# A three-layer graph network kernel: eight groups in flight instead of four, dot products of layers 2 and 3 one slot earlier, small VectorE operations as tensor-tensor

## The chip, the core and the metric

One core of one Trainium2 chip. The time is the device time of one execution in microseconds, from its first to its last instruction with the little that lies around it; the kernel before took 2461.77 us, the median of 3 runs (2460.39 to 2462.76).

## What is computed

128 graphs of 128 nodes with 256 features each. The input is normalized and cut at zero, goes through three graph attention layers, and is added to the untouched input:

```python
mask = adjacency + eye > 0
x = relu(layernorm(x_in))
for l in range(3):
    si, sj = x @ attn_w[l, :d], x @ attn_w[l, d:]
    scores = leaky_relu(si[:, :, None] + sj[:, None, :] + attn_b[l], 0.2)
    attn = softmax(where(mask, scores, -inf))
    h = layernorm(x + attn @ x) * g1[l] + beta1[l]
    ff = gelu(h @ W1[l] + b1[l]) @ W2[l] + b2[l]
    x = layernorm(h + ff) * g2[l] + beta2[l]
return x_in + x
```

## The kernel before, in words

**Items and slots.** Four graphs (T = 4) are one group, and one layer of one group is one item: 32 groups by 3 layers are 96 items. `RING` = 4 groups are in flight: items 0 to 3 are layer 1 of groups 0 to 3, then come four items of layer 2, four of layer 3, and the next four groups. `PER` = 12 items are one round. Every engine runs its own list, written out in Python by `slots`, one slot per item. In slot s every engine goes through c = 0 to 7, the eight blocks of 128 hidden features.

**What a slot holds.** TensorE (`hidden`, L369, and `feed`, L383) does the two large products of item s, each split in fp16 high and low parts; `feed` runs three blocks late (`LAG`), so its last three lie in c = 0 to 2 of the next slot. In between TensorE does small parts of items that come: the aggregation of item s+1 at c = 0 (L425), at c = 4 the transposes of the normalized rows of item s+1 (L435) and the spreading of the s_j of item s+2 (L407), and at c = 7 the transposes of the probabilities of item s+2 (L413).

ScalarE does GELU and the fp16 rounding of each block (L481, L486), the normalization of item s+1 at c = 2 (L491), the high part of X at c = 3 (L528), of hT at c = 4 (L535), at c = 5 the exponentials of item s+2 (`exponentials`: the leaky ReLU L509, then a table load and four exponentials L514), and at c = 7 the normalization of an input.

VectorE does the low part of each block (`g_lo`, L573), after c = 0 the statistics' end of norm 1 (`aggregates`: L585, L587, L588), after c = 1 the eight dot products of item s+2 (`dot_products`, L614 and L617), after c = 2 the residual of the second norm (`feed_residual`, L681), after c = 3 its statistics (L580), after c = 4 the scores (L632), their row maxima (`row_maxima`, L638 and L642) and `aggregates` of norm 2, after c = 5 the low part of hT (L671) and the statistics of an input, after c = 6 the low part of the probabilities and a mask, after c = 7 the residual of the first norm (L656) and its statistics.

GpSimd does, in this order and once per slot: 1/sqrt of norm 1 (`inverse_deviation`, L789 and L791, handed to ScalarE's L491), `h_residual` (L801, L803), the low part of X (`low_X`, L807), 1/sqrt of norm 2, `norm_feed` (four L815), for items of layer 3 the `skip_connection` (L836), for a group that starts 1/sqrt of the input's norm, and `layer_output` (L827, L829, twice).

**What fixes the order.** The lists are written by hand, each engine works through its own in order, and semaphores with computed totals join them. Inputs (`input_statistics`, mask, input normalization) are four slots ahead of their item (`starts`). X of an item in layer 2 or 3 is the output of the item `RING` before it, written by `layer_output` at the end of the slot after that one: with RING = 4, X for item s+3 is the output of item s-1, which is written at the end of slot s. `h_residual` waits, besides its operands, for the dot products of item s+2. The row maxima end in one instruction, `minus_max` = min(0.2 * row_top, row_top), and ScalarE's exponentials wait for it.

SP issues all DMAs in order: weights at the start, then per group the inputs, the store and the second load of x for the skip connection, in buffers used in turn.

Of the kernel before, what the change touches and what calls it, by code (L numbers as in the profile page):

```python
# [41 lines left out]
RING = 4  # L42
# [55 lines left out]

def is_item(r, s):
    return not isinstance(r, int) or 0 <= PER * r + s < ITEMS  # L100
# [29 lines left out]
def gnn_kernel(nc, x, adj, attn_w, attn_b, W1, b1, W2, b2, g1, beta1, g2, beta2, out):  # L130
    with ExitStack() as ctx:
# [12 lines left out]
        minus_half = sb("minus_half", [P, T])  # L144
        w1_f32 = sb("w1_f32", [P, KD, H])
# [21 lines left out]
        x_again = [sb(f"x_again{i}", [P, T, D]) for i in range(2)]  # L167
        y_out = [sb(f"y_out{i}", [P, T, D]) for i in range(2)]
# [106 lines left out]
        def _(sp):  # L275
            def weights(l):
                if l >= 1:
                    sp.wait_ge(w_lo_ready, 4 * l - 2)
                    sp.wait_ge(bias_psum, l)
                sp.dma_start(w1_f32[:], W1[l].rearrange("(k p) h -> p k h", p=P)).then_inc(w_dma[0], 16)  # L280
                if l >= 1:
                    sp.wait_ge(w_lo_ready, 4 * l)
                sp.dma_start(w2_f32[:], W2[l].rearrange("(c p) d -> p c d", p=P)).then_inc(w_dma[1], 16)

            def graphs(tensor, g):

                v = tensor.rearrange("(g t) n d -> n g t d", t=T)
                if isinstance(g, int):
                    return v[:, g]
                return v[:, bass.ds(g, 1)].rearrange("n g t d -> n (g t) d")  # L290

            def load_x(g, i):
                sp.dma_start(x_in[i][:], graphs(x, g)).then_inc(x_loaded[i], 16)

            def load_adj(g, i):
                sp.dma_start(adj_in[i][:], graphs(adj, g)).then_inc(adj_loaded[i], 16)

            def load_again(g, i):
                sp.dma_start(x_again[i][:], graphs(x, g)).then_inc(x_again_loaded[i], 16)

            def store(g, i):
                sp.dma_start(graphs(out, g), y_out[i][:]).then_inc(stored[i], 16)

            load_x(0, 0)
            load_adj(0, 0)
# [7 lines left out]
            load_x(1, 1)  # L313
            load_adj(1, 1)
            weights(0)
            for g in (2, 3, 4, 5):
                sp.wait_ge(x0_ready, 4 * (g - 1))
                load_x(g, g % 2)
                sp.wait_ge(mask_steps, 2 * (g - 1))
                load_adj(g, g % 2)  # L320
                if g == 2:
                    for dst, v in ((g1_rows, g1), (b2_rows, b2), (res_rows, beta1), (g2_rows, g2), (beta2_rows, beta2)):
                        sp.dma_start(dst[:].rearrange("p l d -> p (l d)"),
                                     flat(v).partition_broadcast(P)).then_inc(rows_dma, 16)
                if g in (3, 4):
                    weights(g - RING + 2)
            load_again(0, 0)
            load_again(1, 1)

            for r in range(LOOPS - 1):  # L330
                for q in range(RING):
                    i, g = q % 2, r * RING + q

                    sp.wait_ge(x0_ready, r * (4 * RING) + 4 * (RING + q + 1))
                    load_x(g + (RING + 2), i)
                    sp.wait_ge(mask_steps, r * (2 * RING) + 2 * (RING + q + 1))
                    load_adj(g + (RING + 2), i)

                    sp.wait_ge(x_steps, x_total(r, 2 * RING + q, 5))
                    store(g, i)  # L340
                    load_again(g + 2, i)
            for g in range(RING * (LOOPS - 1), G):
                if g + RING + 2 < G:
                    sp.wait_ge(x0_ready, 4 * (g + RING + 1))
                    load_x(g + RING + 2, g % 2)
                    sp.wait_ge(mask_steps, 2 * (g + RING + 1))
                    load_adj(g + RING + 2, g % 2)
                sp.wait_ge(x_steps, x_total(g // RING, 2 * RING + g % RING, 5))
                store(g, g % 2)
                if g + 2 < G:  # L350
                    load_again(g + 2, g % 2)
# [115 lines left out]
        def _(act):  # L467
# [39 lines left out]
            def exponentials(r, s):  # L507
                act.wait_ge(score_steps, total(r, s, 6, 6))
# [52 lines left out]
        def _(dve):  # L561
# [73 lines left out]
            def row_maxima(r, s):  # L635

                dve.wait_ge(score_steps, total(r, s, 6, 4))
                dve.tensor_reduce(row_top[:], scores[:], AX.X, ALU.max, negate=True).then_inc(score_steps, 1)  # L638
                dve.wait_ge(score_steps, total(r, s, 6, 5))
# [66 lines left out]
            def slot(r, s):  # L706
# [7 lines left out]
                for c in range(C):  # L714
# [35 lines left out]
                    if c == 5 and starts and not late:  # L750
                        input_statistics(r, s + 4)
# [127 lines left out]
```

## Time and profile before

| | |
|---|---|
| median of the runs | 2461.77 us |
| the profiled execution | 2464.22 us, span 2462.4 us |
| busy: TensorE matmul | 2350.7 us (95%) |
| VectorE | 2097.8 us (85%) |
| ScalarE | 1890.0 us (77%) |
| GpSimd | 1701.0 us (69%) |
| DMA | 29 GB/s mean, the queue 9.1% busy |
| granted TensorE clock | 0.993 over the span |

The profiled execution lies 2.4 us above the median of the runs. A matmul's row gives 273 ns where the next one starts 0.11 us later, since matmuls overlap: TensorE's rate is read from the start-to-start times in its timeline, and a gap from the start of the last matmul before it.

### The profile page before, as it was taken

What the parts mean: (1) busy time and instruction counts of PE and PEld (TensorE: products, weight loads), DVE (VectorE), ACT (ScalarE), POOL (GpSimd) and SP (SyncE); (2) the same over time, 40 slices, a digit from 0 to 9 for tenths busy, and PEclk for the clock granted to TensorE, in tenths of its full rate; (3) what the DMA queues carried; (4) which work ended last, traced back from release to release, by engine and by line L of the source; (5) the groups of instructions that cost most, each with busy time, mean ns of one, the idle gap of its engine ahead of it and who ended that gap; (6) DMA issues with size and microseconds to landing.
All of it is one profiled execution on the core that took longest, in us unless ns stands there. A gap on an engine that the chain in (4) does not pass through costs nothing.

```text
span 2462.4 us, 47718 instructions
## 1 busy us (share of the span) xinstructions
PE 2350.7 (95%) x16608; PEld 1648.4 (67%) x16608; DVE 2097.8 (85%) x6070; ACT 1890.0 (77%) x3402; POOL 1701.0 (69%) x1540
## 2 busy tenths in 40 slices
PE   3999999999999999999999999999999999999997
PEld 2766666676666666667666666666666666666765
DVE  6778998888988899888988889988898889988884
ACT  4767788877787878787787777877778777878783
POOL 3457677767776767766786667776678676777675
PEclk9999999999999999999999999999999999999998
DMA  5200012000210002100021001200012000110001
GB/s 170 73 1 1 1 44 78 1 1 1 74 48 1 1 14 61 48 1 1 14 78 31 1 1 31 73 18 2 1 44 61 18 2 1 44 52 1 1 1 52
DMA packets 77422, 70.84 MB, mean 29 GB/s; under 512 B 7040, under 2 KB 75648, under 8 KB 77184
## 3 DMA queue, kind: packets, MB, share of 16 engines
q1 hardware_dynamic: 77184, 67.79, 9.1%
q8 instruction: 134, 2.20, 0.4%
q14 instruction: 104, 0.85, 0.1%
HBM read 51.01 MB, written 16.78 MB: 28 GB/s over the span
## 4 chain that ended last, share of the span: by engine, by line
DVE 55%; PE 19%; ACT 13%; issue 10%; POOL 0%; DVEq 0%; POOLq 0%
DVE g_lo L573 11%; DVE bn L580 9%; PE p_pair L383 8%; DVE res L656 6%; DVE dots L614 6%; ACT probs L514 5%; PE p_hid L369 5%; ACT L514 5%; DVE res L681 5%; DVE scores L632 4%; DVE dots L617 4%; PE p_pair L425 3%; DVE row_top L638 3%; DVE minus_max L642 2%; PE p_att L413 2%
## 5 line engine op out<-in xcount | busy, mean ns | idle before, releaser
L383 PE MATMUL p_pair<-w_hi,g_hi 128*128 128x256 f16 x3072 | 839.1, 273 | 0.0
L383 PE MATMUL p_pair<-w_lo,g_hi 128*128 128x256 f16 x3072 | 838.8, 273 | 0.0
L383 PE MATMUL p_pair<-w_hi,g_lo 128*128 128x256 f16 x3072 | 838.8, 273 | 0.0
L481 ACT ACTIVATE p_hid<-p_hid,b_eff 128x512 f32<-128x512 f32 x768 | 504.5, 657 | 328.6 <-PE p_hid L369 327.4
L573 DVE TENSOR_TENSOR g_lo<-p_hid,g_hi 128x512 f16<-128x512 f32 x768 | 527.5, 687 | 239.4 <-ACT g_hi L486 232.9
L801 POOL TENSOR_TENSOR h_res<-norm,g_rows 128x1024 f32<-128x1024 f32 x96 | 227.7, 2372 | 395.8 <-DVE res L681 389.1
L486 ACT ACTIVATE g_hi<-p_hid 128x512 f16<-128x512 f32 x768 | 458.5, 597 | 24.3
L369 PE MATMUL p_hid<-hT_hi,w_hi 128*128 128x512 f16 x1536 | 458.7, 380 | 2.3 <-DVE g_lo L573 2.3
L369 PE MATMUL p_hid<-hT_hi,w_lo 128*128 128x512 f16 x1536 | 458.9, 380 | 0.0
L369 PE MATMUL p_hid<-hT_lo,w_hi 128*128 128x512 f16 x1536 | 458.8, 380 | 0.0
L789 POOL TENSOR_TENSOR rstd<-var_eps,minus_half 128x4 f32<-128x4 f32 x224 | 241.6, 1079 | 307.4 <-DVE minus_mean L588 302.1
L383 PEld LDWEIGHTS p_pair<-w_lo,g_hi 128*128 128x128 f16 x3072 | 301.2, 98 | 107.3 <-issue 0.8
L383 PEld LDWEIGHTS p_pair<-w_hi,g_hi 128*128 128x128 f16 x3072 | 301.2, 98 | 106.2 <-issue 1.0
L383 PEld LDWEIGHTS p_pair<-w_hi,g_lo 128*128 128x128 f16 x3072 | 301.2, 98 | 35.5
L491 ACT ACTIVATE norm<-res,shift,rstd 128x256 f32<-128x256 f32 x384 | 199.3, 589 | 102.0 <-POOL shift L791 102.0
L369 PEld LDWEIGHTS p_hid<-hT_lo,w_hi 128*128 128x128 f16 x1536 | 150.8, 98 | 182.6 <-issue 2.5
L369 PEld LDWEIGHTS p_hid<-hT_hi,w_lo 128*128 128x128 f16 x1536 | 150.7, 98 | 182.5 <-issue 2.2
L580 DVE BATCH_NORM_STATS2 bn<-res 128x6 f32<-128x256 f32 x768 | 268.9, 414 | 3.3
L803 POOL TENSOR_TENSOR h_res<-h_res,res_rows 128x1024 f32<-128x1024 f32 x96 | 226.9, 2363 | 7.5
L587 DVE TENSOR_SCALAR var_eps<-mv 128x4 f32<-128x4 f32 x224 | 213.4, 953 | 7.7
L815 POOL TENSOR_SCALAR norm<-res,rstd,shift 128x256 f32<-128x256 f32 x384 | 209.8, 561 | 10.0
L656 DVE SCALAR_TENSOR_TENSOR res<-p_pair,row_inv,X 128x256 f32<-128x256 f32 x384 | 159.0, 477 | 65.5 <-PE p_pair L425 65.5
(67 smaller groups left out, 3855.2 us busy)
## 6 DMA issues: line engine op xcount, KB each, us to landing
x_in<-in_x SPq DMA_DIRECT2D x32, 512.0 KB, 5.3
x_again<-in_x SPq DMA_DIRECT2D x32, 512.0 KB, 5.1
out<-y_out SPq DMA_DIRECT2D x32, 512.0 KB, 3.3
adj_in<-in_adj SPq DMA_DIRECT2D x32, 256.0 KB, 5.6
w_f<-in_L_gnn_W SPq DMA_DIRECT2D x6, 1024.0 KB, 5.6
attn_rows<-in_L_gnn_attn_w SPq DMA_DIRECT2D x1, 768.0 KB, 5.6
g_rows<-in_L_gnn_g SPq DMA_DIRECT2D x2, 384.0 KB, 8.3
b_rows<-in_L_gnn_b SPq DMA_DIRECT2D x1, 384.0 KB, 7.4
```

Of the source, the lines that this page charges most:

```text
L369: mm = pe.matmul(p_hid[in_ring(s, c, PF_RING)][:], w[l][:, k, cols], h[i][:, k, :], start=(n == 0), stop=(n == 3 * KD - 1))
L383: mm = pe.matmul(ff_banks(s)[:, t, :], g[i][:, nodes], w[l][:, c, :], start=(c == 0 and t % 2 == 0 and n == 0), stop=(c == C - 1 and n == ...
L481: act.activation(p_hid[k][:], p_hid[k][:], ACT.Gelu, bias=b1_eff[:, l, c:c + 1], scale=1.0 / WSCALE).then_inc(gelu_ready, 1)
L486: act.activation(g_hi[i][:], p_hid[k][:], ACT.Copy).then_inc(g_hi_ready, 1)
L514: act.activation(probs[:, t, :], leaky[:, t, :], ACT.Exp, bias=minus_max[:, t:t + 1], accum_out=row_sum[:, t:t + 1]).then_inc(probs_ready, 1)
L573: dve.tensor_tensor(g_lo[i][:], p_hid[k][:], g_hi[i][:], ALU.subtract).then_inc(g_lo_ready, 1)
L580: dve.bn_stats(bn[n][:, t, :], src[:, t, :]).then_inc(stat_steps[n], 1)
L587: dve.tensor_scalar(var_eps[n][:], mv[n][:, :, 1], EPS, None, ALU.add).then_inc(stat_steps[n], 1)
L656: dve.scalar_tensor_tensor(out=res1[:, t, :], in0=agg_banks(s)[:, t, :], scalar=row_inv[:, t:t + 1], in1=X[s % RING][:, t, :], op0=ALU.mul ...
L789: pool.tensor_tensor(rstd[n][s % 2][:], var_eps[n][:], minus_half[:], ALU.pow).then_inc(rstd_ready[n], 1)
L801: pool.tensor_tensor(h_res[i][:], norm1[:], rows(g1_rows, l, T), ALU.mult).then_inc(h_res_steps, 1)
L803: pool.tensor_tensor(h_res[i][:], h_res[i][:], rows(res_rows, l, T), ALU.add).then_inc(h_res_steps, 1)
```

## The change

Three things, and what they need.

1. `RING` is 8: eight items of layer 1, eight of layer 2, eight of layer 3; a round is 24 items. X for item s+3 is now the output of item s-5. Inputs, masks and input normalizations come in runs of eight slots instead of four. To have room, `y_out` and `x_again` lie in the fp32 buffers of the weights, which are free once the weights are split; GpSimd waits for that once, and SP's list is rewritten slot by slot.
2. The dot products of items of layers 2 and 3 move from c = 1 of slot s (item s+2) to c = 5 (item s+3), after the low part of hT. Those of layer 1 stay. GpSimd waits for these dot products ahead of 1/sqrt of norm 2, and `skip_connection` moves to the front of that wait.
3. `var_eps` and `minus_mean` (L587, L588) become tensor-tensor operations against constant tiles that GpSimd fills at the start, and `minus_max` (L642) becomes two tensor-tensor operations with a wait on the first between them.

```diff
-RING = 4
+RING = 8
...
-        x_again = [sb(f"x_again{i}", [P, T, D]) for i in range(2)]
-        y_out = [sb(f"y_out{i}", [P, T, D]) for i in range(2)]
+        y_out = [w1_f32[:, i, :].rearrange("p (t d) -> p t d", t=T) for i in range(2)]
+        x_again = [w2_f32[:, i * T:(i + 1) * T, :] for i in range(2)]
...
+            def slot(r, s):
+                if is_item(r, s + 2) and layer_of(s + 2) == 0 and group_of(r, s + 2) + 2 < G:
+                    sp.wait_ge(x0_ready, group_total(r, s + 2, 4, 4))
+                    load_x(group_of(r, s + 2) + 2)
+                if is_item(r, s + 3) and layer_of(s + 3) == 0 and group_of(r, s + 3) + 2 < G:
+                    sp.wait_ge(mask_steps, group_total(r, s + 3, 2, 2))
+                    load_adj(group_of(r, s + 3) + 2)
...
+                if is_item(r, s - 3) and layer_of(s - 3) == L - 1:
+                    store(r, s - 3)
...
-                dve.tensor_scalar(var_eps[n][:], mv[n][:, :, 1], EPS, None, ALU.add).then_inc(stat_steps[n], 1)
-                dve.tensor_scalar(minus_mean[n][:], mv[n][:, :, 0], -1.0, None, ALU.mult).then_inc(stat_steps[n], 1)
+                dve.tensor_tensor(var_eps[n][:], mv[n][:, :, 1], eps_row[:], ALU.add).then_inc(stat_steps[n], 1)
+                dve.tensor_tensor(minus_mean[n][:], mv[n][:, :, 0], minus_one[:], ALU.mult).then_inc(stat_steps[n], 1)
...
-                dve.scalar_tensor_tensor(out=minus_max[:], in0=row_top[:], scalar=SLOPE, in1=row_top[:],
-                                         op0=ALU.mult, op1=ALU.min).then_inc(score_steps, 1)
+                dve.tensor_tensor(minus_max[:], row_top[:], slope_row[:], ALU.mult).then_inc(score_steps, 1)
+                dve.wait_ge(score_steps, total(r, s, 7, 6))
+                dve.tensor_tensor(minus_max[:], minus_max[:], row_top[:], ALU.min).then_inc(score_steps, 1)
...
-                    if c == 1 and is_item(r, s + 2):
+                    if c == 1 and is_item(r, s + 2) and layer_of(s + 2) == 0:
...
+                    if c == 5 and is_item(r, s + 3) and layer_of(s + 3) > 0:
+
+                        dot_products(r, s + 3, 0)
+                        dot_products(r, s + 3, 1)
...
+                if is_item(r, s - 2) and layer_of(s - 2) == L - 1:
+                    skip_connection(r, s - 2)
                 if is_item(r, s - 1):
+                    if is_item(r, s + 3) and layer_of(s + 3) > 0:
+
+                        pool.wait_ge(dots_ready, total(r, s + 3, 8, 8))
                     inverse_deviation(s - 1, 2, total(r, s - 1, 10, 10), total(r, s - 1, 2, 1))
                     norm_feed(r, s - 1)
-                if is_item(r, s - 2) and layer_of(s - 2) == L - 1:
-                    skip_connection(r, s - 2)
```

VectorE before, from the row maxima of item s+2 to the second block after them, in a slot without a starting group:

```order
L638 TENSOR_REDUCE row_top<-scores 128x4 [waits score_steps]
L642 SCALAR_TENSOR_TENSOR minus_max<-row_top 128x4 [waits probs_ready,score_steps]
L585 BN_AGGR mv<-bn 128x2 x4
L587 TENSOR_SCALAR var_eps<-mv 128x4 [waits stat_steps2]
L588 TENSOR_SCALAR minus_mean<-mv 128x4
L573 TENSOR_TENSOR g_lo<-p_hid,g_hi 128x512 [waits g_hi_ready]
L671 TENSOR_TENSOR hT_lo<-p_pair,hT_hi 128x1024 [waits hT_hi_ready]
L573 TENSOR_TENSOR g_lo<-p_hid,g_hi 128x512 [waits g_hi_ready]
```

And the same place of the changed kernel, in a slot whose item s+3 is of layer 2 or 3 (an ISA row is a dot product or the read of its sum):

```order
L635 TENSOR_REDUCE row_top<-scores 128x4 [waits score_steps]
L639 TENSOR_TENSOR minus_max<-row_top,slope_row 128x4 [waits probs_ready,score_steps]
L641 TENSOR_TENSOR minus_max<-minus_max,row_top 128x4 [waits score_steps]
L582 BN_AGGR mv<-bn 128x2 x4
L584 TENSOR_TENSOR var_eps<-mv,eps_row 128x4 [waits stat_steps2]
L585 TENSOR_TENSOR minus_mean<-mv,minus_one 128x4
L570 TENSOR_TENSOR g_lo<-p_hid,g_hi 128x512 [waits g_hi_ready]
L669 TENSOR_TENSOR hT_lo<-p_pair,hT_hi 128x1024 [waits hT_hi_ready]
L611 ISA dots,s_i<-X,attn_rows,attn_b_col 128x256 [waits x_steps]
L611 ISA s_i 128x1
L614 ISA dots,s_j<-X,attn_rows 128x256
L614 ISA s_j 128x1
```

The maxima take one instruction more, with a wait, and the eight dot products stand behind hT_lo instead of in front of `feed_residual`.

GpSimd before, from 1/sqrt of norm 1 on, in a slot with a skip connection:

```order
L789 TENSOR_TENSOR rstd_0<-var_eps,minus_half 128x4 [waits stat_steps1]
L791 TENSOR_TENSOR shift_0<-minus_mean,rstd_0 128x4 [waits rstd_ready1]
L801 TENSOR_TENSOR h_res<-norm,g_rows 128x1024 [waits res2_ready,dots_ready,norm1_ready]
L803 TENSOR_TENSOR h_res<-h_res,res_rows 128x1024 [waits h_res_steps]
L807 TENSOR_TENSOR X_lo<-X,X_hi 128x1024 [waits X_hi_ready]
L789 TENSOR_TENSOR rstd_0<-var_eps,minus_half 128x4 [waits stat_steps2]
L791 TENSOR_TENSOR shift_0<-minus_mean,rstd_0 128x4 [waits rstd_ready2]
L815 TENSOR_SCALAR norm<-res,rstd_0,shift_0 128x256 [waits x_steps,rstd_ready2]
L815 TENSOR_SCALAR norm<-res,rstd_0,shift_0 128x256 x3
L836 TENSOR_TENSOR y_out<-y_out,x_again 128x1024 [waits x_again_loaded1,x_steps]
```

And now (w_f is the old weight buffer that holds y_out and x_again):

```order
L795 TENSOR_TENSOR rstd_0<-var_eps,minus_half 128x4 [waits stat_steps1]
L797 TENSOR_TENSOR shift_0<-minus_mean,rstd_0 128x4 [waits rstd_ready1]
L807 TENSOR_TENSOR h_res<-norm,g_rows 128x1024 [waits res2_ready,dots_ready,norm1_ready]
L809 TENSOR_TENSOR h_res<-h_res,res_rows 128x1024 [waits h_res_steps]
L813 TENSOR_TENSOR X_lo<-X,X_hi 128x1024 [waits X_hi_ready]
L844 TENSOR_TENSOR w_f<-w_f 128x1024 [waits x_again_loaded1,x_steps]
L795 TENSOR_TENSOR rstd_0<-var_eps,minus_half 128x4 [waits stat_steps2]
L797 TENSOR_TENSOR shift_0<-minus_mean,rstd_0 128x4 [waits rstd_ready2]
L821 TENSOR_SCALAR norm<-res,rstd_0,shift_0 128x256 [waits x_steps,rstd_ready2]
```

The skip connection stands right behind `low_X` now.

## Rows read from the trace of the kernel before

**Rows 1.** VectorE's timeline (start us, us, engine, line): the row maxima, once per slot

```profile
410.50 0.69 DVE L638 TENSOR_REDUCE row_top<-scores 128x4 f32<-128x512 f32 x1
...
581.07 0.69 DVE L638 TENSOR_REDUCE row_top<-scores 128x4 f32<-128x512 f32 x1
...
606.66 0.69 DVE L638 TENSOR_REDUCE row_top<-scores 128x4 f32<-128x512 f32 x1
```

**Rows 2.** Groups of instructions by form (count | busy us, mean ns | idle before)

```profile
L369 PE MATMUL p_hid<-hT_lo,w_hi 128*128 128x512 f16 x1536 | 458.8, 380 | 0.0
...
L836 POOL TENSOR_TENSOR y_out<-y_out,x_again 128x1024 f32<-128x1024 f32 x31 | 72.8, 2348 | 0.0
```

**Rows 3.** TensorE's timeline in a slot without a starting group

```profile
472.51 0.59 PE L369 MATMUL p_hid<-hT_hi,w_hi 128*128 128x512 f16 x2
...
480.33 1.04 PE L435 MATMUL p_pair<-ident,norm 128*128 128x128 f32 x8
...
487.71 0.59 PE L369 MATMUL p_hid<-hT_lo,w_hi 128*128 128x512 f16 x2
488.55 0.66 PE L413 MATMUL p_att<-ident,probs 128*128 128x128 f32 x4 [0.25 <-ACT probs L514]
```

**Rows 4.** VectorE's timeline in the same slot and the one before

```profile
460.84 1.77 DVE L587 TENSOR_SCALAR var_eps<-mv 128x4 f32<-128x4 f32 x1
...
463.19 1.21 DVE L671 TENSOR_TENSOR hT_lo<-p_pair,hT_hi 128x1024 f16<-128x1024 f32 x1
...
475.01 0.48 DVE L614 CUSTOM_DVE_ANT_0 dots<-X,attn_rows,attn_b_col 128x256 bf16<-128x256 f32 x1
...
478.61 1.28 DVE L681 SCALAR_TENSOR_TENSOR res<-p_pair,h_res 128x512 f32<-128x512 f32 x2
...
482.44 1.12 DVE L632 SCALAR_TENSOR_TENSOR scores<-p_att,s_i,mask 128x128 f32<-128x128 f32 x4
483.59 0.69 DVE L638 TENSOR_REDUCE row_top<-scores 128x4 f32<-128x512 f32 x1
484.31 0.56 DVE L642 SCALAR_TENSOR_TENSOR minus_max<-row_top 128x4 f32<-128x4 f32 x1
```

**Rows 5.** ScalarE's timeline in the same slot

```profile
475.92 2.08 ACT L491 ACTIVATE norm<-res,shift,rstd 128x256 f32<-128x256 f32 x4 [0.62 <-POOL shift L791]
...
478.56 0.60 ACT L486 ACTIVATE g_hi<-p_hid 128x512 f16<-128x512 f32 x1
...
480.69 0.60 ACT L486 ACTIVATE g_hi<-p_hid 128x512 f16<-128x512 f32 x1
...
483.83 0.60 ACT L486 ACTIVATE g_hi<-p_hid 128x512 f16<-128x512 f32 x1
484.91 0.63 ACT L509 ACTIVATE leaky<-scores 128x512 f32<-128x512 f32 x1 [0.48 <-DVE minus_max L642]
```

**Rows 6.** GpSimd's timeline in the same slot and the one before

```profile
462.76 1.02 POOL L789 TENSOR_TENSOR rstd<-var_eps,minus_half 128x4 f32<-128x4 f32 x1 [0.17 <-DVE minus_mean L588]
...
470.21 1.27 POOL L829 TENSOR_TENSOR X<-X,beta_rows 128x512 f32<-128x512 f32 x1
474.58 1.02 POOL L789 TENSOR_TENSOR rstd<-var_eps,minus_half 128x4 f32<-128x4 f32 x1 [3.10 <-DVE minus_mean L588]
...
480.06 2.36 POOL L801 TENSOR_TENSOR h_res<-norm,g_rows 128x1024 f32<-128x1024 f32 x1 [4.17 <-DVE res L681]
482.50 2.35 POOL L803 TENSOR_TENSOR h_res<-h_res,res_rows 128x1024 f32<-128x1024 f32 x1
484.81 2.13 POOL L807 TENSOR_TENSOR X_lo<-X,X_hi 128x1024 f16<-128x1024 f32 x1
```

**Rows 7.** VectorE's timeline in an early slot: the same instruction, and it took longer

```profile
159.56 1.92 DVE L642 SCALAR_TENSOR_TENSOR minus_max<-row_top 128x4 f32<-128x4 f32 x1
```

**Rows 8.** GpSimd's timeline at the same moment

```profile
159.34 2.12 POOL L807 TENSOR_TENSOR X_lo<-X,X_hi 128x1024 f16<-128x1024 f32 x1
```

**Rows 9.** The instructions of line 642: duration ns min/median/max

```profile
L642 DVE SCALAR_TENSOR_TENSOR minus_max<-row_top x96: 161/557/1919, 27.9 to 2391.6; 128x4 f32<-128x4 f32 x96
```

More of the change, by code:

```diff
@@ L275, in _, with weights @@
         def _(sp):
-            def weights(l):
+            def weights(l, n):
                 if l >= 1:
-                    sp.wait_ge(w_lo_ready, 4 * l - 2)
+                    sp.wait_ge(w_lo_ready, 4 * l - 2 + 2 * n)
+                if l >= 1 and n == 0:
                     sp.wait_ge(bias_psum, l)
[L280 to L283, printed above, removed]
+                if n == 0:
+                    sp.dma_start(w1_f32[:], W1[l].rearrange("(k p) h -> p k h", p=P)).then_inc(w_dma[0], 16)
+                else:
+                    sp.dma_start(w2_f32[:], W2[l].rearrange("(c p) d -> p c d", p=P)).then_inc(w_dma[1], 16)
@@ L301, in store, with load_x, load_adj, load_again @@
[L301 to L305, printed above, removed]
+                return tensor.rearrange("(g t) n d -> n g t d", t=T)[:, g]
+            def load_x(g):
+                sp.dma_start(x_in[g % 2][:], graphs(x, g)).then_inc(x_loaded[g % 2], 16)
+            def load_adj(g):
+                sp.dma_start(adj_in[g % 2][:], graphs(adj, g)).then_inc(adj_loaded[g % 2], 16)
+            def load_again(g):
+                sp.dma_start(x_again[g % 2], graphs(x, g)).then_inc(x_again_loaded[g % 2], 16)
@@ new lines, in store @@
+            def store(r, s):
+                g = group_of(r, s)
+                sp.wait_ge(x_steps, x_total(r, s, 5))
+                sp.dma_start(graphs(out, g), y_out[g % 2]).then_inc(stored[g % 2], 16)
+                if g + 2 < G:
+                    load_again(g + 2)
+            def slot(r, s):
[5 more added lines that the diff above has]
+                    load_adj(group_of(r, s + 3) + 2)
+                if (r, s) == (0, -2):
+                    for dst, v in ((g1_rows, g1), (b2_rows, b2), (res_rows, beta1), (g2_rows, g2), (beta2_rows, beta2)):
+                        sp.dma_start(dst[:].rearrange("p l d -> p (l d)"),
+                                     flat(v).partition_broadcast(P)).then_inc(rows_dma, 16)
+                if (r, s) in ((0, -1), (0, 1)):
+                    weights((s + 3) // 2, 0)
+                if is_item(r, s - 3) and layer_of(s - 3) == L - 1:
+                    store(r, s - 3)
+                if (r, s) in ((0, -1), (0, 1)):
+                    weights((s + 3) // 2, 1)
+                if (r, s) == (0, 5):
+                    sp.wait_ge(w_lo_ready, 4 * L)
+                    load_again(0)
+                    load_again(1)
@@ L312, in _ @@
                     sp.dma_start(dst[:], v.rearrange("l (c p) -> p l c", p=P)).then_inc(cols_dma, 16)
[L313 to L351, printed above, removed]
+            load_x(1)
+            load_adj(1)
+            weights(0, 0)
+            weights(0, 1)
+            slots(sp, slot)
+            for s in range(PER - 2, PER):
+                store(LOOPS, s)
             for i in range(2):
@@ L821, in layer_output @@
                 dst = y_out[q % 2] if l == L - 1 else X[q]
+                if l == L - 1 and not later(r, s, 2 * RING + 2):
+                    pool.wait_ge(w_lo_ready, 4 * L)
                 if l == L - 1 and later(r, s, 2 * RING + 2):
```

29 lines of the change are left out of this document (14 added, 15 removed).

## The prediction, on record before the changed kernel ran

> **What bounds the kernel now.** I read the length of a slot first, since a matmul's row is longer than its turn and TensorE's busy share says little. VectorE's row maxima come once per slot: seven slots from 410.50 to 581.07 are 24.37 us each, the next, in which a group starts, is 25.59 [rows 1]. Slots 4 to 92 hold 61 of the first length and 28 of the second, 2203 us; the rest is start and end.
>
> How much of a slot is TensorE's own? One matmul of 512 columns shows 0.38 us [rows 2], two in a row 0.59 [rows 3], so they start 0.21 apart, and those at 487.71 let the next start at about 488.14. The transposes of the probabilities start at 488.55, released by ScalarE: a gap of 0.41. It is the only one in this slot, so TensorE alone would need 23.96 us. In slots with a starting group a second gap, ahead of the transposes of norm 1, makes up the rest.
>
> What ends last at this gap is one chain: scores 482.44, row maxima 483.59, minus_max 484.31 for 0.56 us [rows 4], leaky ReLU at 484.91 [rows 5], transposes 3.64 us later [rows 3]. ScalarE is free for it at 483.83 + 0.60 = 484.43, and its row says that it waits 0.48 for minus_max. So the gap goes if minus_max is done by 484.45, and grows by all that minus_max is later than 484.87.
>
> Why do four elements take 0.56 us? GpSimd's second h_res instruction ends at 482.50 + 2.35 = 484.85, minus_max at 484.87 [rows 4, 6]. And in an early slot the same instruction started at 159.56, after low_X at 159.34, and took 1.92 us, to 161.48; low_X ended at 161.46 [rows 7, 8]. A VectorE instruction with both inputs in SBUF waited for GpSimd's to end. var_eps, with one input, did so too: 460.84 for 1.77 us [rows 4].
>
> I count from H = 472.51, the start of block 2 [rows 3]. minus_max starts at H+11.80 and ends at H+12.36.
>
> **The dot products.** Eight of them lie from 475.01 to about 478.01, and a block's low part of 0.6 us stands between them and feed_residual at 478.61 [rows 4]: 3.0 us leave this place. But feed_residual's release of GpSimd's h_res is then no longer last: h_res also needs norm 1, which ScalarE ends at 475.92 + 2.08 = 478.00 [rows 5]. So h_res starts at H+5.55 instead of H+7.55 (480.06 [rows 6]), and with 2.36 + 2.35 + 2.13 us and their small spaces low_X runs from H+10.30 to H+12.42. The scores come little earlier, since their block's g_hi ends at 480.69 + 0.60 = 481.29 [rows 5]: low part, scores and row maxima put minus_max at H+11.33 instead of H+11.80. It now falls into low_X, as in the early slot [rows 7, 8], where it fell on the end of h_res.
>
> **minus_max as two instructions.** No row of the kernel before shows a small tensor-tensor operation with both inputs in SBUF beside a long GpSimd one. Bounds: below, it never waits, and two of 0.16 (its shortest row [rows 9]) with a wait of 0.05 between them end at about H+11.7. Above, each waits for a whole GpSimd instruction. The nearest row is minus_max as it was, same tiles, same size, two inputs in SBUF, and it waited [rows 4, 7]; I take that. Then the first ends with low_X at H+12.45, the second follows at once where GpSimd has nothing more to run, at H+12.66, 0.30 later than now. The Trainium skill, "SBUF — State Buffer", section "Who interferes with whom", goes further than these rows: it says of tensor_tensor with both inputs in SBUF that it contends with GpSimd's reads although it has no 2-port mode. By that the sum is the same.
>
> **GpSimd's new wait.** It waits for the moved dot products before 1/sqrt of norm 2. VectorE gets to them after minus_max, the aggregates (0.6), a low part (0.6) and hT_lo (1.15, from 463.19 [rows 4]): H+15.05, done at H+18.05. From rstd 2 to the end of the layer output is 471.48 - 462.76 = 8.72 us [rows 6]: H+26.9. The next 1/sqrt of norm 1 is wanted 2.07 after the next H (474.58 [rows 6]), H+26.73. GpSimd had 3.10 us to spare there [rows 6]; that is used up, and it is late by about 0.35. In all a slot of this kind is 24.37 + 0.30 + 0.35 = 25.0 us. There are 48: 1200 us.
>
> **The skip connection** (2.35 us [rows 2]) now stands right behind low_X, and minus_max's second instruction, some 0.05 us after the first, finds it running, as the row of 159.56 found low_X. It ends 2.3 us later: 27.3 us, 12 slots, 328 us.
>
> **Slots whose dot products stay at c = 1** (layer 1). h_res stays where it is, the first instruction ends at H+12.36 as now, the second meets low_X, which runs from 484.81 to 486.94 [rows 6]: 2.1 us more, 26.5 us. There are 8 of these in each of three rounds and 2 at the start. Ahead of each eight lies one slot of about 29: the slot before it has an input's statistics, the dot products and GpSimd's wait for them. Three times 8 x 26.5 + 29 = 241 is 723 us, the 2 are 53.
>
> **The start.** Slots 0 to 3 get four more inputs among the splitting of weights: between nothing (ScalarE waits there) and four normalizations of 2.08 us [rows 5]; I take 4. The loads move with them, four slots ahead as before, and cost nothing. The constants of GpSimd are three fills, hidden behind the first load. var_eps gains nothing in time: after c = 4 it lies under the exponentials, after c = 0 GpSimd is now at its layer output or just done.
>
> **The sum.** 1200 + 328 + 723 + 53 = 2304 against 2203, and 4 at the start: 105 us more. From the profiled execution's 2464.2 this gives 2569, and that lay 2.4 above the median of the runs: **2567 us**. This case by itself reaches from 2505 (GpSimd not late, the skip connection missed half the time) to 2615 (every maxima pair behind one more GpSimd instruction).
>
> **Rival 1, the other side: small tensor-tensor operations do not wait for GpSimd.** For it: the waits seen are of a one-input tensor-scalar and a scalar-tensor-tensor instruction, none of a tensor-tensor [rows 4, 7]. Against it: two inputs are read either way. Then minus_max ends at H+11.7, ScalarE is free at H+11.92, the transposes could start at H+15.6, and TensorE gets to them at H+15.63: no gap. GpSimd's chain, with dots ending at H+17.1, is done at H+25.9, when it is wanted at H+26.03. 60 slots of 23.96 are 1438 us. In the three runs of nine, an input's 1/sqrt makes GpSimd 0.8 late: seven of 24.7, one of 25.9, one of 24.2, together 223 each; the 2 at the start 49. That is 2156, 47 less than now; with 4 at the start and the 2.4 it is **2419 us**. The point from which it decides: minus_max's second instruction ending before H+11.9. The Trainium skill, "VectorE: DVE Perf Modes", section "Why `tensor_tensor` can't do 2×_2P or 4×", read alone speaks for this rival, since it rules a 2-port mode out for this operation. The same section gives the second read port to the second tensor, which speaks against it.
>
> **Rival 2: the first waits, the second never does,** since it gets in between two GpSimd instructions. Then low_X costs +0.2 and 0.35 in 60 slots (33 us), and the 29 others keep about 24.8 (nothing gained or lost): 2462 + 33 + 4, **2499 us**. Against it: GpSimd's next instruction starts 0.04 us before the last one's row ends (484.81 against 484.85 [rows 6]), too soon for that.
>
> **Rival 3: gains and losses cancel.** The waits fall only on some slots, and the rest reach 23.96: **2462 us**. Nothing in the rows speaks for such a mixture, as every slot of one kind runs alike.
>
> **Chances.** My case 0.50, rival 2 and what lies between it and my case 0.10, rival 1 0.35, rival 3 0.05. I give rival 1 that much because no row shows the operation itself. A measurement here can tell 0.2% from no change, some 5 us. Faster is rival 1 and a little of rival 3, 0.36; same is the middle of rival 3, 0.03; slower is the rest, 0.61. The range has to reach both sides: rival 1 down to 2410, my case up to 2610.
>
> **What would show it.** Right: minus_max's first instruction at some 1.1 us beside low_X, the second at 2.2 beside the skip connection; leaky ReLU waiting 0.8 us or more for it; TensorE's gap ahead of the transposes of the probabilities at 0.8 to 3 us; GpSimd waiting for the s_j of the dot products. Wrong: small tensor-tensor rows of 0.16 to 0.2 us beside a long GpSimd row, and row maxima 23.96 us apart.

## The result: 2599.63 us, 5.6% slower, and the profile after

The changed kernel takes 2599.63 us, the median of 4 runs (2596.57 to 2603.6), beside 2461.77 (2460.39 to 2462.76) for the kernel before. The ratio is 1.0559, with a 95% interval of 1.0546 to 1.0573. The forecast was 2567, from 2410 to 2610: the sign and the mechanism came as foretold, the size 33 us short. That the time lies in the range says little by itself, since the range was drawn to hold rival 1's 2419 as well; the rows below are the test.

The head of the page of the changed kernel, with the first lines of its chain of waits:

```profile
span 2599.0 us, 47820 instructions
PE 2380.5 (92%) x16608; PEld 1665.1 (64%) x16608; DVE 2114.7 (81%) x6166; ACT 1888.9 (73%) x3402; POOL 1701.1 (65%) x1543
...
DVE 39%; PE 22%; ACT 22%; issue 11%; POOL 5%; DVEq 0%; ACTq 0%; POOLq 0%
```

No engine has much more to do than before: GpSimd's busy time is the same to 0.1 us, VectorE's is 17 us up, TensorE's 30 with the same number of matmuls, while the span grew by 137. The time is mostly in waits. The waits of the changed kernel (engine and line, what it waited for, us in total, times, longest):

```profile
POOL rstd L795 <- DVE s_j L614: 358.4, 64, 6.7
...
ACT leaky L506 <- DVE minus_max L641: 184.4, 93, 9.2
PE p_att L410 <- ACT probs L511: 164.7, 94, 4.8
POOL h_res L807 <- ACT norm L488: 144.3, 66, 2.2
POOL h_res L807 <- DVE res L679: 120.6, 29, 4.2
```

The second and third are the chain of the prediction, minus_max to leaky ReLU to the transposes of the probabilities. TensorE waits at its end in 94 of 96 slots, now 164.7 / 94 = 1.75 us a time. The first is GpSimd's new wait. The last two show h_res released by norm 1 in the slots with moved dot products and by feed_residual in the others, as worked out.

**A slot with moved dot products.** VectorE's timeline of the changed kernel (start us, us, engine, line), answering to [rows 1] and [rows 4]:

```profile
974.40 1.12 DVE L629 SCALAR_TENSOR_TENSOR scores<-p_att,s_i,mask 128x128 f32<-128x128 f32 x4
975.55 0.69 DVE L635 TENSOR_REDUCE row_top<-scores 128x4 f32<-128x512 f32 x1
976.27 1.11 DVE L639 TENSOR_TENSOR minus_max<-row_top,slope_row 128x4 f32<-128x4 f32 x1
977.42 0.16 DVE L641 TENSOR_TENSOR minus_max<-minus_max,row_top 128x4 f32<-128x4 f32 x1
...
1000.40 0.69 DVE L635 TENSOR_REDUCE row_top<-scores 128x4 f32<-128x512 f32 x1
```

GpSimd's timeline at the same place, answering to [rows 6]:

```profile
972.92 2.36 POOL L809 TENSOR_TENSOR h_res<-h_res,res_rows 128x1024 f32<-128x1024 f32 x1
975.23 2.14 POOL L813 TENSOR_TENSOR X_lo<-X,X_hi 128x1024 f16<-128x1024 f32 x1
982.95 1.02 POOL L795 TENSOR_TENSOR rstd<-var_eps,minus_half 128x4 f32<-128x4 f32 x1 [5.59 <-DVE s_j L614]
```

Low_X ends at 977.37, the first maxima instruction at 977.38: a small tensor-tensor instruction waits for GpSimd's. The second follows in its shortest time, and the slot is 1000.40 - 975.55 = 24.85 us, where 25.0 was forecast.

**A slot with a skip connection.** VectorE and then GpSimd of the changed kernel, a few slots earlier in a round:

```profile
543.28 1.10 DVE L639 TENSOR_TENSOR minus_max<-row_top,slope_row 128x4 f32<-128x4 f32 x1
544.42 2.28 DVE L641 TENSOR_TENSOR minus_max<-minus_max,row_top 128x4 f32<-128x4 f32 x1
...
542.25 2.12 POOL L813 TENSOR_TENSOR X_lo<-X,X_hi 128x1024 f16<-128x1024 f32 x1
544.33 2.34 POOL L844 TENSOR_TENSOR w_f<-w_f 128x1024 f32<-128x1024 f32 x1
```

**A slot whose dot products stay at c = 1** (slot 23, which has a skip connection and a starting group as well). The same two engines:

```profile
683.50 0.56 DVE L639 TENSOR_TENSOR minus_max<-row_top,slope_row 128x4 f32<-128x4 f32 x1
684.09 2.05 DVE L641 TENSOR_TENSOR minus_max<-minus_max,row_top 128x4 f32<-128x4 f32 x1
686.06 0.37 DVE L582 BATCH_NORM_AGGREGATE mv<-bn 128x2 f32<-128x6 f32 x4
686.46 1.98 DVE L584 TENSOR_TENSOR var_eps<-mv,eps_row 128x4 f32<-128x4 f32 x1
...
681.68 2.35 POOL L809 TENSOR_TENSOR h_res<-h_res,res_rows 128x1024 f32<-128x1024 f32 x1
683.99 2.13 POOL L813 TENSOR_TENSOR X_lo<-X,X_hi 128x1024 f16<-128x1024 f32 x1
686.07 2.35 POOL L844 TENSOR_TENSOR w_f<-w_f 128x1024 f32<-128x1024 f32 x1
```

Each of three small instructions ends with the GpSimd instruction that was running: 684.03, 686.12 and 688.42 on GpSimd, 684.06, 686.14 and 688.44 on VectorE. In this slot TensorE's row at the transposes of the probabilities says that it waited 2.65 us for them, where it says 0.25 in [rows 3].

**Where the 137 us are**, from the row maxima of slot s to those of slot s+1 (us in all). A slot is put in its row by what stands in front of and beside its maxima:

| slots | before | forecast | after |
|---|---|---|---|
| 48: no dot products at c = 1, no skip connection (6 to 17, 30 to 41, 54 to 65, 78 to 89) | 1190.7 | 1200 | 1192.8 |
| 12: no dot products at c = 1, a skip connection (18, 19, 21, 42, 43, 45, 66, 67, 69, 90 to 92) | 296.1 | 328 | 334.6 |
| 27: slots 20, 44 and 68, and the 8 with dot products at c = 1 of each round (22 to 29, 46 to 53, 70 to 77) | 669.2 | 723 | 752.9 |
| 2 at the start with dot products at c = 1 (4, 5) | 48.7 | 53 | 54.2 |
| slots 0 to 3 | 112.2 | 116 | 115.6 |
| span from the last row maxima | 71.5 | 71.5 | 74.4 |

The first row comes out level because 16 of the 28 starting groups before, at 25.59 a slot or a little more, lay in these slots, which now have none: 24.81 a slot in the mean before, 24.85 now.

**TensorE's clock** took a share that the prediction has no term for. Three slots of the changed kernel (stretch, its length, busy us of TensorE, its weight loads, VectorE, ScalarE and GpSimd, then TensorE's granted clock, the DMA share and GB/s; slots 22, 25 and 34):

```profile
655.07:682.76 27.69, 24.64 (x177) 17.20 (x175) 26.45 (x72) 21.00 (x40) 20.36 (x19) 1.00 0.21 68
738.15:766.27 28.12, 25.47 (x172) 17.23 (x170) 25.49 (x73) 20.65 (x38) 20.36 (x19) 0.94 0.21 67
975.55:1000.40 24.85, 24.11 (x174) 16.95 (x173) 19.98 (x61) 18.92 (x35) 16.41 (x16) 1.00 0.00 1
```

In the middle one, TensorE's timeline has a gap of 2.65 us, and then rows of 0.42 us where they had been 0.27:

```profile
745.18 0.66 PE L410 MATMUL p_att<-ident,probs 128*128 128x128 f32 x4 [2.65 <-ACT probs L511]
746.33 0.28 PE L380 MATMUL p_pair<-w_hi,g_hi 128*128 128x256 f16 x1
746.44 0.39 PE L380 MATMUL p_pair<-w_lo,g_hi 128*128 128x256 f16 x1
746.62 0.42 PE L380 MATMUL p_pair<-w_hi,g_lo 128*128 128x256 f16 x1
746.83 0.42 PE L380 MATMUL p_pair<-w_hi,g_hi 128*128 128x256 f16 x1
```

They start 0.21 apart instead of 0.11: the lower of the clock's two levels (1.2 instead of 2.4 GHz), for some 3.4 us (0.94 over 28.12 us is 3.4 us at half the clock). This slot is 0.43 us longer than the one at full clock above; among skip slots, 28.4 was measured instead of 26.96 (42, 43, 90 and 91). Slots 21, 45 and 69, with a gap of 4.8 us and a clock of 0.94, took 28.7.

Of the executions behind this text one was disturbed, the profiled one of experiment 4 (10150 us, at a granted clock of 0.235 over the span); only its first thirty slots, at their usual lengths, are read.

### The profile page after: what moved, and what is told of

Its sections match the earlier page's. It is cut to its first block, busy times and chain, and to the rows that moved or that the text cites. A ratio compares the mean times of both kernels' runs of the same rounds, so it can differ in the third digit from the quotient of the medians.

```text
span 2599.0 us, 47820 instructions
## 1 busy us (share of the span) xinstructions
PE 2380.5 (92%) x16608; PEld 1665.1 (64%) x16608; DVE 2114.7 (81%) x6166; ACT 1888.9 (73%) x3402; POOL 1701.1 (65%) x1543
## 4 chain that ended last, share of the span: by engine, by line
DVE 39%; PE 22%; ACT 22%; issue 11%; POOL 5%; DVEq 0%; ACTq 0%; POOLq 0%
PE p_pair L380 10%; DVE res L654 6%; PE p_hid L366 5%; DVE bn L577 5%; DVE g_lo L570 5%; ACT probs L511 5%; ACT L511 4%; ACT norm L488 4%; DVE scores L629 4%; PE p_pair L422 4%; DVE minus_max L641 4%; DVE minus_max L639 3%; ACT p_hid L478 3%; POOL rstd L795 3%; DVE row_top L635 2%
## 5 line engine op out<-in xcount | busy, mean ns | idle before, releaser
L380 PE MATMUL p_pair<-w_hi,g_hi 128*128 128x256 f16 x3072 | 849.0, 276 | 0.0
L380 PE MATMUL p_pair<-w_lo,g_hi 128*128 128x256 f16 x3072 | 848.7, 276 | 0.0
L380 PE MATMUL p_pair<-w_hi,g_lo 128*128 128x256 f16 x3072 | 848.2, 276 | 0.0
L410 PE MATMUL p_att<-ident,probs 128*128 128x128 f32 x384 | 69.4, 308 | 164.7 <-ACT probs L511 164.7
L821 POOL TENSOR_SCALAR norm<-res,rstd,shift 128x256 f32<-128x256 f32 x384 | 210.8, 563 | 10.1 <-POOL shift L797 0.2
```

The lines of the kernel that those rows point to most:

```text
L380: mm = pe.matmul(ff_banks(s)[:, t, :], g[i][:, nodes], w[l][:, c, :], start=(c == 0 and t % 2 == 0 and n == 0), stop=(c == C - 1 and n == ...
```

## The experiments

Row maxima to row maxima is the length of a slot in each. The number behind a time is its ratio to the kernel before, measured beside it, with the 95% interval. A light slot is one without a starting group and without a skip connection.

**1. The changed kernel with one scalar-tensor-tensor instruction for the maxima.**

```diff
...
-                dve.tensor_tensor(minus_max[:], row_top[:], slope_row[:], ALU.mult).then_inc(score_steps, 1)
-                dve.wait_ge(score_steps, total(r, s, 7, 6))
-                dve.tensor_tensor(minus_max[:], minus_max[:], row_top[:], ALU.min).then_inc(score_steps, 1)
+                dve.scalar_tensor_tensor(out=minus_max[:], in0=row_top[:], scalar=SLOPE, in1=row_top[:],
+                                         op0=ALU.mult, op1=ALU.min).then_inc(score_steps, 1)
```

> The changed kernel with minus_max as one scalar-tensor-tensor instruction again. Theory W (a VectorE instruction with two inputs in SBUF waits for the GpSimd instruction beside it, and the second operation of minus_max pays this a second time): the first still ends with low_X, the second wait is gone. Slots with moved dot products 24.65 to 24.85 us, also those with a skip connection; slots whose dot products stay, 25.6 or 24.4 as before the change. About 2485 us (2470 to 2510). Rival D (the moved dot products, GpSimd's new wait and eight groups in flight cost the time): stays within 20 us of 2600.

Measured: 2509.17 us, 1.0193 (1.0178 to 1.0208), at the upper edge of what was expected. Slots with moved dot products are 24.68 us, slots 20, 44 and 68 still 29.44, most others of those runs 25.6. The second instruction is worth 90 us of the 138. The remaining 47 come with the moved dot products and GpSimd's new order: the single instruction, now inside low_X, takes 1.11 us where the one before took 0.56. Skip slots are 26.3 and not the 24.85 at most that was expected, because another two-input instruction now meets the skip connection. GpSimd and VectorE in slot 18:

```profile
536.84 2.36 POOL L843 TENSOR_TENSOR w_f<-w_f 128x1024 f32<-128x1024 f32 x1
...
537.23 1.99 DVE L584 TENSOR_TENSOR var_eps<-mv,eps_row 128x4 f32<-128x4 f32 x1
```

var_eps waits to 539.22, the skip connection ends at 539.20, and the dot products stand behind var_eps. In the changed kernel the second maxima instruction bears this wait, and var_eps behind it takes 0.16. In experiment 6, where var_eps comes early enough to meet low_X instead (0.82 us), the skip connection stands in the same place and these slots are 24.35.

**2. The kernel before with the two maxima instructions and nothing else** (the diff of experiment 1 the other way, with the constant tiles).

> The kernel before with nothing changed but minus_max as two tensor-tensor operations. Theory W: the first ends with the second h_res instruction, the second meets low_X and ends 2.1 us later, in all of some 93 slots: 2462 + 195 = 2657 us (2640 to 2670), the row of the second at 2.05 us. Rival D: 2462 to 2470 us, both rows at 0.16 to 0.6 us.

Measured: 2694.11 us, 1.0946 (1.0927 to 1.0964), 37 us above what was expected and worse than the whole change. Light slots are 26.44 us, as the expected sum had them, but about every second one is 28.1. Two neighbours:

```profile
1123.09:1151.14 28.05, 25.73 (x174) 17.95 (x172) 20.91 (x60) 19.09 (x35) 16.39 (x16) 0.94 0.00 1
1151.14:1177.58 26.44, 24.13 (x175) 16.96 (x173) 20.92 (x61) 19.01 (x35) 16.41 (x16) 1.00 0.00 1
```

And TensorE's timeline in the first of them:

```profile
1130.12 1.11 PE L414 MATMUL p_att<-ident,probs 128*128 128x128 f32 x4 [2.32 <-ACT probs L515]
1131.03 0.42 PE L384 MATMUL p_pair<-w_hi,g_hi 128*128 128x256 f16 x1
1131.24 0.42 PE L384 MATMUL p_pair<-w_lo,g_hi 128*128 128x256 f16 x1
```

After the gap the rows are those of the lower clock, and the slot pays 1.6 us more. So the two instructions alone cost more in the old order than in the new: there the first ends with h_res and the second meets all of low_X, while the moved dot products bring GpSimd forward by 2 us, so that the pair meets one instruction and not two.

**3. The kernel before with var_eps and minus_mean as tensor-tensor.**

```diff
...
-                dve.tensor_scalar(var_eps[n][:], mv[n][:, :, 1], EPS, None, ALU.add).then_inc(stat_steps[n], 1)
-                dve.tensor_scalar(minus_mean[n][:], mv[n][:, :, 0], -1.0, None, ALU.mult).then_inc(stat_steps[n], 1)
+                dve.tensor_tensor(var_eps[n][:], mv[n][:, :, 1], eps_row[:], ALU.add).then_inc(stat_steps[n], 1)
+                dve.tensor_tensor(minus_mean[n][:], mv[n][:, :, 0], minus_one[:], ALU.mult).then_inc(stat_steps[n], 1)
```

> The kernel before with nothing changed but var_eps and minus_mean as tensor-tensor operations. Theory W: a tensor-tensor operation waits like the tensor-scalar one, rows of 1.2 and 1.8 us stay: 2462 us within 4. Rival F (the form frees the two from the wait): the 28 slots with a starting group lose 1.0 us at their first 1/sqrt: 2434 us, rows of 0.16 us.

Measured: 2462.1 us, 1.0001 (0.9992 to 1.0011). Nothing, and the rows say why: var_eps takes over 1 us in 119 of its 224 runs in either kernel, and 1.77 us at most in either, so both forms wait alike.

**4. The changed kernel with low_X held back until minus_max is done.**

```diff
                 if is_item(r, s + 1):
+                    pool.wait_ge(score_steps, total(r, s + 2, 7, 7))
...
```

> The changed kernel with one wait more: GpSimd starts low_X only when minus_max of the same item is done. Theory W: nothing of GpSimd runs beside the two operations in slots with moved dot products, both rows 0.16 us, these slots come to 24.0 us where there is no skip connection; the others keep at most the wait on the second h_res instruction (0.5 us). 2420 to 2455 us. Rival D: the two rows stay long or other work takes their place, above 2540 us.

Measured: 1.0315 (1.0297 to 1.0332), some 2539 us: far from the 2420 to 2455 that was expected, and near the other side, where other work takes the place of the two rows. VectorE's and GpSimd's timelines in one slot:

```profile
365.73 0.16 DVE L639 TENSOR_TENSOR minus_max<-row_top,slope_row 128x4 f32<-128x4 f32 x1
365.93 0.16 DVE L641 TENSOR_TENSOR minus_max<-minus_max,row_top 128x4 f32<-128x4 f32 x1
366.01 0.37 DVE L582 BATCH_NORM_AGGREGATE mv<-bn 128x2 f32<-128x6 f32 x4
366.42 1.90 DVE L584 TENSOR_TENSOR var_eps<-mv,eps_row 128x4 f32<-128x4 f32 x1
...
366.17 2.13 POOL L813 TENSOR_TENSOR X_lo<-X,X_hi 128x1024 f16<-128x1024 f32 x1 [1.44 <-DVE minus_max L641]
373.21 1.02 POOL L795 TENSOR_TENSOR rstd<-var_eps,minus_half 128x4 f32<-128x4 f32 x1 [4.91 <-DVE s_j L614]
```

The maxima are free at 0.16 each. But low_X starts 0.25 us before var_eps, which then pays 1.90, and behind it in VectorE's list are the dot products for which GpSimd waits. The slot is 25.43 us, longer than the 24.85 without the wait: the price moved from a chain on TensorE's path to a loop VectorE to GpSimd to ScalarE's norm 1 and back. Experiment 9 puts the wait at var_eps to the test.

**5. The changed kernel without GpSimd's wait for the dot products.**

```diff
-                    if is_item(r, s + 3) and layer_of(s + 3) > 0:
-
-                        pool.wait_ge(dots_ready, total(r, s + 3, 8, 8))
```

> The changed kernel without GpSimd's wait for the moved dot products. Theory W: the waits of minus_max stay, so most of the loss stays; GpSimd is no longer late at its next 1/sqrt of norm 1, which gives back at most the 0.2 us per slot that slots with moved dot products lie above 24.65, and the dot products' rows grow where GpSimd's normalization runs beside them: 2575 to 2605 us. Rival D (GpSimd's new wait is the main cost): 2480 us or less.

Measured: 2607.11 us, 1.0589 (1.0572 to 1.0607), just above what was expected; slots of 25.01 instead of 24.85. Freed, norm_feed runs beside the dot products: the four L821 take 3.45 us instead of 2.16 and dot products 0.68 instead of 0.48, one of them 1.48. So taking the wait out does not pay; it keeps two things apart that hinder each other.

**6 and 7. No minus_max at all**, in the changed kernel (6) and in the kernel before (7). This leaves out the factor 0.2 and the minimum: the exponentials are shifted by the raw row maximum, which cancels in the softmax. It does so as long as the exponentials stay in range: where a row's raw maximum m is negative, the largest of them is exp(-0.8 m) and not 1. The cut is experiment 7's; in 6 the two tensor-tensor instructions go.

```diff
...
-                dve.scalar_tensor_tensor(out=minus_max[:], in0=row_top[:], scalar=SLOPE, in1=row_top[:],
-                                         op0=ALU.mult, op1=ALU.min).then_inc(score_steps, 1)
...
-                    act.activation(probs[:, t, :], leaky[:, t, :], ACT.Exp, bias=minus_max[:, t:t + 1],
+                    act.activation(probs[:, t, :], leaky[:, t, :], ACT.Exp, bias=row_top[:, t:t + 1],
```

> The changed kernel without minus_max: the exponentials take minus the maximum of the raw scores (row_top) as their shift, which cancels in the softmax. Theory W: nothing waits there any more; slots with moved dot products about 24.1 us (24.5 with a skip connection), set by the loop over dot products, GpSimd's wait and 1/sqrt of norm 1; the others 24.4 to 25.2. About 2437 us (2420 to 2465). Rival D: above 2500.

> The kernel before without minus_max in the same way. If the chain over minus_max sets TensorE's gap there, slots without a starting group come to TensorE's own 23.96 us and the others lose 0.4: 2461 - 61 x 0.4 - 28 x 0.4 = 2426 us (2420 to 2440). If another chain is just behind it, above 2450.

Measured: 2434.86 us, 0.9889 (0.9874 to 0.9904) for the first, as expected, and 2417.16, 0.9813 (0.9798 to 0.9828) for the second, 9 us better than the 2426 expected and 3 below its range. That is 1.9% faster than the kernel before. Without the maxima's small operation the changed kernel is 165 us faster, and all else in the change together costs 18 us. In the kernel before, light slots become 23.90 us, TensorE's own 23.96 of the prediction. Experiment 7 beats both kernels.

**8. Eight groups in flight and SP's new list, nothing else.**

```diff
-RING = 4
+RING = 8
...
```

> The kernel before with eight groups in flight and the rewritten SP list and nothing else: dot products, small operations, GpSimd's order as before. Theory W: four slots with a starting group fewer among slots 4 to 92 (5 us less), four more at the start (4 to 8 us more): 2461 us within 6. Rival D: a good part of the 138 us, 2500 or more.

Measured: 2462.05 us, 0.9998 (0.9988 to 1.0007). The new order of groups and loads is free on balance: slots 0 to 3 are 3 us longer, and 24 starting groups instead of 28 lie among slots 4 to 92.

**9. The changed kernel with low_X behind minus_max and the aggregates of norm 2.**

```diff
                 if is_item(r, s + 1):
+                    pool.wait_ge(score_steps, total(r, s + 2, 7, 7))
+                    if is_item(r, s - 1):
+                        pool.wait_ge(stat_steps[2], total(r, s - 1, 10, 10))
```

> The changed kernel, but GpSimd starts low_X only when minus_max and the two small operations of norm 2's aggregates are done. Theory W with the loop (minus_max, aggregates, hT_lo, dot products, GpSimd's wait, its 8.7 us, 1/sqrt of norm 1): in slots with moved dot products nothing waits ahead of the dot products, 24.1 us; with a skip connection the dot products and GpSimd's instructions wait for each other, 25.5; slots whose dot products stay, 24.6 and 25.9. Sum 2465 us (2445 to 2485). If the wait that the run before showed at var_eps was not what held the loop, slots with moved dot products stay at 25.4 and the time at 2540.

Measured: 2490.84 us, 1.0118 (1.0104 to 1.0131), 6 us above the expected range. Slots with moved dot products are 24.35 us. VectorE's and GpSimd's timelines:

```profile
384.90 0.16 DVE L584 TENSOR_TENSOR var_eps<-mv,eps_row 128x4 f32<-128x4 f32 x1
...
386.79 0.89 DVE L611 CUSTOM_DVE_ANT_0 dots<-X,attn_rows,attn_b_col 128x256 bf16<-128x256 f32 x1
387.61 0.41 DVE L614 CUSTOM_DVE_ANT_0 dots<-X,attn_rows 128x256 bf16<-128x256 f32 x1
...
385.27 2.13 POOL L813 TENSOR_TENSOR X_lo<-X,X_hi 128x1024 f16<-128x1024 f32 x1 [2.05 <-DVE minus_mean L585]
390.37 1.02 POOL L795 TENSOR_TENSOR rstd<-var_eps,minus_half 128x4 f32<-128x4 f32 x1 [2.97 <-DVE s_j L614]
```

var_eps is back at 0.16, and only the first dot product, begun before low_X ends (387.40), takes 0.89 instead of 0.48. Slots go from 25.43 to 24.35: the loss of experiment 4 sat in var_eps, at least in these slots. The price of a GpSimd instruction can be made small by choosing which VectorE instruction meets it. The kernel is still slower than the one before, mostly by slots 20, 44 and 68 (28.29) and the skip slots (26.27).

**10. Experiment 7 with the skip connection in front of h_residual.**

```diff
+                if is_item(r, s - 2) and layer_of(s - 2) == L - 1:
+                    skip_connection(r, s - 2)
+                if is_item(r, s + 1):
...
-                if is_item(r, s - 2) and layer_of(s - 2) == L - 1:
-                    skip_connection(r, s - 2)
```

> The kernel before without minus_max, and GpSimd's skip connection moved into its idle time between 1/sqrt of norm 1 and h_residual. Theory: slots with both a starting group and a skip connection (25.45 us) lose the lateness that the skip connection gives the layer output, and come to the 25.0 of those without: 14 x 0.45 = 6 us less than the 2417 of the run without minus_max, 2411 us (2405 to 2418). If h_residual comes later for it, 2417 or more.

Measured: 2479.53 us, 1.0075 (1.0062 to 1.0088), a clear miss. GpSimd, VectorE and TensorE in a skip slot:

```profile
375.75 2.61 POOL L833 TENSOR_TENSOR y_out<-y_out,x_again 128x1024 f32<-128x1024 f32 x1
...
376.07 2.57 DVE L617 CUSTOM_DVE_ANT_0 dots<-X,attn_rows 128x256 bf16<-128x256 f32 x1
...
382.00 1.76 PE L435 MATMUL p_pair<-ident,norm 128*128 128x128 f32 x7 [2.86 <-DVE res L678]
```

The dot products at c = 1 also stop for it: 2.57 us instead of 0.41, and TensorE waits 2.86 for the residual behind them.

**11 and 12. The changed kernel without minus_max, low_X behind the aggregates, the skip connection in front of h_residual**: in all slots (11), or only where the dot products are not at c = 1 (12). Both shift by the raw maximum, as 6 and 7. Experiment 12 adds to 11:

```diff
+                dots_here = is_item(r, s + 2) and layer_of(s + 2) == 0
...
-                if is_item(r, s - 2) and layer_of(s - 2) == L - 1:
+                if is_item(r, s - 2) and layer_of(s - 2) == L - 1 and not dots_here:
                     skip_connection(r, s - 2)
...
+                if is_item(r, s - 2) and layer_of(s - 2) == L - 1 and dots_here:
+                    skip_connection(r, s - 2)
```

> The changed kernel without minus_max, GpSimd's skip connection between 1/sqrt of norm 1 and h_residual, and low_X after the small operations of norm 2's aggregates. Theory: nothing waits for GpSimd on the way to the dot products but low_X's last 0.4 us: 24.05 us in slots with moved dot products, 24.6 in slots with a starting group: about 2412 us (2400 to 2430). If the loop over the dot products has another wait, 2435 or more as in the run without minus_max alone.

> The kernel of the run before with eight groups in flight, no minus_max and low_X behind the aggregates, but the skip connection goes ahead of h_residual only in slots whose dot products do not stand at c = 1, and behind norm 2's application in the others. Theory: the slots of 27 to 29 us there were dot products that waited for the skip connection (row of 2.57 us); they come to 25.2, which is 3 x 10 us less than 2443: 2412 us (2405 to 2425). If those slots had another cause, above 2435.

Measured: 2443.55 us, 0.9929 (0.9917 to 0.9942) for 11, a miss: all slots with moved dot products, those with a skip connection too, are at 23.9 us, but slots 20 to 24 are 26.5 to 29, by the mechanism of experiment 10, and the same in the two rounds behind; in all it is 9 us slower than experiment 6. And 2421.75 us, 0.9827 (0.9813 to 0.9840) for 12, as expected. Experiment 7 is without the eight groups, the moved dot products, GpSimd's new order and waits, and the new form of the statistics. Beside it, the 60 slots of the first two rows of the table take 1437 us and not 1458, since the starting groups lie elsewhere; the 27 of the third row take 681 and not 657, and slots 0 to 3 are 8 us longer. What is won in one place is lost in the others, and the two kernels are level: their intervals overlap.

## Why the prediction was right, and where its size was off

**The chain that ends last: right.** minus_max, leaky ReLU and the transposes set the gap; taking minus_max away gives 45 us in the kernel before and 165 in the changed one.

**A small tensor-tensor instruction waits for GpSimd's running one: right,** and this decided the sign. Rival 1 wanted rows of 0.16 to 0.2 beside a long GpSimd row and slots of 23.96; the rows are 1.10, 2.05 and 2.28 us. No run has the maxima as one tensor-tensor instruction or as two of the old form, so that the form itself plays no part is read from rows alone: inside low_X the single scalar-tensor-tensor instruction took 1.11 us (experiment 1), the first tensor-tensor one 1.11. What was cited of the Trainium skill, "SBUF — State Buffer", section "Who interferes with whom", holds by these rows. What the Trainium skill says in "VectorE: DVE Perf Modes", section "Why `tensor_tensor` can't do 2×_2P or 4×", of the missing 2-port mode alone misled towards rival 1: a tensor-tensor operation without that mode took 2.28 us.

**Rival 2, the second slips in between: refuted** by 544.42 for 2.28 us. GpSimd's skip connection had started at 544.33, before the first maxima instruction ended. **Rival 3, gains and losses cancel: refuted** by every class of slots but the first of the table.

**Slots with moved dot products: 24.85 for 25.0,** right to 0.15. The 0.15 is a slip in the sum: GpSimd's work done at H+26.9 and wanted at H+26.73 makes it 0.17 late, where 0.35 stood, and 24.37 + 0.30 + 0.17 is 24.84. In 48 slots that is 7 us, against the shortfall of the others. The first maxima instruction ends with low_X and the second follows at once, as worked out. With the maxima free and the loop still closed, experiment 9 has 24.35.

**Skip slots: right in size where the clock did not fall** (26.96 for 27.3 in five of the twelve). Four are at 28.4 with the clock at 0.94, and slots 21, 45 and 69, which have a starting group too, at 28.7 with the same clock. The twelve together are 7 us above the forecast.

**Slots whose dot products stay at c = 1: the step that was mis-sized.** "2.1 us more, 26.5 us" added the wait to 24.37, the length of a slot without a starting group. But six of the eight slots of each round (22 to 27, 46 to 51, 70 to 75) have a starting group, and I had read 25.59 for these [rows 1]. Experiment 2 and the changed kernel both show that the 2.1 comes on top: 27.68 and 27.69, and the light slot 28 is 26.44. With 25.6 + 2.1 = 27.7 in 18 slots the sum gains some 21 us. Slots 20, 44 and 68 were 29.91 where 29 stood: 3 us more. The rest of the 30 us, some 6, lies in slots in which the granted clock fell.

**The clock: missing from the sum.** The gaps that the prediction foretold, up to 3 us, were priced at their length alone. The clock that falls behind some of them is worth another 12 us or so here: 1.45 in each of four skip slots, and the 6 above; what it has in slots 21, 45 and 69 can't be told from the other things in them. In experiment 2 every second light slot pays it.

**The start and the loads: right.** 3.4 us for 4; experiment 8 has eight groups and the new list of loads at nothing on balance, experiment 3 the statistics' operations. **The tail was left out:** 2.9 us.

**The new wait: half right.** GpSimd waits 358 us in all for the dot products, but without the wait the kernel is no faster (experiment 5). So the lateness, 0.17 by the figures above, is that of a loop (experiments 4 and 9) and not a price of the wait.

**Luck.** The errors of the terms have both signs: the 48 slots came 7 us below the forecast, the others and the tail 40 above, and only the difference is the 33 us of the result.

## What to carry to other kernels

Before splitting a small VectorE operation or choosing its form, look at which long GpSimd instruction runs beside it: four elements cost the rest of that instruction, and two dependent ones can cost two of them. The cheapest repair was to need no such operation on the path (a shift that the softmax cancels while its exponentials stay in range, 45 us), the next to say with a semaphore which VectorE instruction the GpSimd one may meet, after looking at what comes next in VectorE's list. And a per-slot cost is added to the length of that kind of slot, never to the shortest.

## What the runs showed of the hardware that was not expected

- The wait is not only for small operations: a dot product with two inputs in SBUF went from 0.41 to 2.57 us beside the skip connection (experiment 10), var_eps with one input took 1.77 [rows 4]. Scores and row maxima, the statistics, g_lo and hT_lo did not stretch beside the same GpSimd instructions: 1.12 us for the scores, begun 1.48 us into h_res at 974.40.
- It works both ways: beside the dot products GpSimd's four normalizations took 3.45 us for 2.16.
- The granted clock fell behind some of TensorE's gaps and not behind others of the same length: behind 34 of 89 of 2.3 to 2.65 us in experiment 2, 15 of 38 of 2.3 to 2.9 in the changed kernel, the three of 4.8 there, and none of 13 of 1.9 in experiment 1. Length alone does not decide: in experiment 2 it fell behind 32 of 67 of 2.31 to 2.34 us, but behind 2 of 22 of 2.64 and 2.65. What tells them apart stays open.
